# Scattering the experts' rows to token order, and moving the middle variance and the rank products beside the next item's embedding

## The chip, the cores and the metric

One core of one Trainium2 chip runs the kernel. The metric is the device time of one execution in microseconds (us). Engines are named as in the profile: PE (TensorE), DVE (VectorE), ACT (ScalarE), POOL (GpSimd), and SP, which here only issues DMAs.

## What is computed

128 images of 176x208 go through a small vision network in float32. `h` is a row of 128 features for each of 144 tokens an image (143 patches and a class token), 18432 tokens in all.

```python
h = tok(x)                        # patches @ W + b, class token, positions
h = h + L0_attn(layernorm(h))     # projections, 4-tap causal convolution, linear scan
                                  #   s[t] = a * s[t-1] + d[t], gates, output projection
h = h + L0_ffn(layernorm(h)):
    x = LN(x + mean over r of repeat(pool(x, 2**r)) @ mr_w[r])   # "middle" normalization
    x = LN(x + sum over v of alpha[v] * gelu(x @ mv_w[v]))
    logits = x @ gate_w + gate_b;  top 2 of 8 experts, softmax of the two
    moe = sum over the two: weight * (gelu(x @ w1[e] + b1[e]) @ w2[e] + b2[e])
    x = LN(x + moe)
h = h + L1_attn(layernorm(h))     # 8 heads, window of 32 tokens to each side
h = h + L1_ffn(layernorm(h))      # one of 16 matrices per image, chosen by the mean
```

## The kernel before

The kernel is three stages in a row. All engines have instruction streams of their own, written out by hand and joined by semaphores. Features lie on the 128 partitions and tokens along the free dimension. An item is 4 images, 576 tokens (`T`), and there are 32.

**Stage A** (`a_tensor`, `a_scalar`, `a_vector`, `a_pool`, `a_sync`) runs a software pipeline without loops: `a_steps` calls each engine's `step(x, y, z, w)` with four successive items. x is embedded and gets its projections, y its scan's end, output projection and middle normalization, z its three views, third normalization and routing. Four double banks of PSUM (`A0`, `A1`, `B0`, `B1`) hold all products, so the order on PE is also the order in which banks come free. In a step, `embed` (24 matmuls, L508) comes near the start. `ranks` (L543 to 555) and the middle variance of y (L656 to 660) come at the end, around the last `unit_in`. `ranks` counts with 14 small matmuls how many earlier tokens chose each expert. On DVE the routing of z is a chain of small operations on 96x48 numbers (`route_first` to `route_weights`, L934 to 1009), placed between the operations of x: `route_ranks` and `route_slots` turn ranks into row numbers (`slot`, `slot_i`), `route_weights` makes the two softmax weights. Row numbers and weights of all items also stay in SBUF, in `slots` and `weights`. POOL adds a residual, multiplies for x (`drive`, L1015, twice), adds (L1031), and then scatters z's rows, 12 indirect DMAs of 96 rows of 128 floats (L1039), into the DRAM tensor `expert_in`, where each expert has a region. ACT changes its function table at four places of a step and names the gelu table twice.

**Stage B** (`b_tensor`, `b_scalar`, `b_vector`, `b_sync`) runs over 152 blocks of 256 rows of one expert each, in a hardware loop with four blocks a round. `b_sync` loads rows and the expert's weights (`w_blk`) and stores the results in block order to `expert_out`. PE turns the next block's rows (L1156), does four hidden products (L1165) and the outputs (L1174). ACT does gelu. DVE copies the turned rows to `x_t` (L1273) and adds the bias into `rows_out` (L1281). Ahead of the loop DVE works out in a chain where each token's two results will lie (`out_rows`, L1261 to 1269).

**Stage C** (`c_tensor`, `c_scalar`, `c_vector`, `c_pool`, `c_sync`) is again a pipeline without loops, `step(v, w, x, y, z)` with five items. For v, SP loads `h1c` and `x2c`, DVE copies v's row numbers to `place` (L1829), and POOL gathers the two results of each token with 12 indirect DMAs (L1466), multiplies them with their weights (L1474) and adds the two (L1479, `ysum`). PE turns the sum (L1509) at the end of the step. w is normalized, giving `xq` (L1961), x has attention in nine units (scores L1538, exponentials L1752, turned L1555, values L1568 and L1580), y and z the last layer. Keys are evicted by ACT at L1737.

## Time and profile before

| what | value |
|---|---|
| time, median of 3 runs | 3334.4 us (3329.47 to 3344.37) |
| the profiled execution's own time | 3318.28 us |
| its span, first to last instruction | 3316.4 us |
| mean granted TensorE clock | 0.901 of full |
| PE busy | 2775.0 us (84%) |
| DVE busy | 1901.2 us (57%) |
| ACT busy | 1843.2 us (56%) |
| POOL busy | 1134.6 us (34%) |
| moved by DMA | 287.14 MB, mean 87 GB/s |

Times in a profile are of one execution. "Busy" is time inside instructions; a wait is booked as idle time ahead of an instruction, with what ended it in brackets. A clock of 1.00 is 2.4 GHz and 0.50 is 1.2 GHz.

### The profile page before, as it was taken

What the parts mean: (1) busy time and instruction counts of PE and PEld (TensorE: products, weight loads), DVE (VectorE), ACT (ScalarE), POOL (GpSimd) and SP (SyncE); (2) the same over time, 40 slices, a digit from 0 to 9 for tenths busy, and PEclk for the clock granted to TensorE, in tenths of its full rate; (3) what the DMA queues carried; (4) which work ended last, traced back from release to release, by engine and by line L of the source; (5) the groups of instructions that cost most, each with busy time, mean ns of one, the idle gap of its engine ahead of it and who ended that gap; (6) DMA issues with size and microseconds to landing.
All of it is one profiled execution on the core that took longest, in us unless ns stands there. A gap on an engine that the chain in (4) does not pass through costs nothing.

```text
span 3316.4 us, 69976 instructions
## 1 busy us (share of the span) xinstructions
PE 2775.0 (84%) x25687; PEld 2181.5 (66%) x25687; DVE 1901.2 (57%) x4527; ACT 1843.2 (56%) x3725; POOL 1134.6 (34%) x964
## 2 busy tenths in 40 slices
PE   6999999999999859999996677877788777877787
PEld 4766666666666549999995456655566555655565
DVE  4878878878788742222221355655565555655566
ACT  4777777777777734444443345544454444544454
POOL 1454555655555530000002533333333333333310
PEclk9999999999999979999998688887888888878888
DMA  3222222222222137777774111111111111111110
GB/s 119 88 84 72 96 83 72 101 78 75 100 76 73 42 114 228 228 230 227 230 228 140 34 40 41 29 41 44 44 40 27 43 44 43 40 28 44 44 30 26
DMA packets 139758, 287.14 MB, mean 87 GB/s; under 512 B 25440, under 2 KB 82784, under 8 KB 135392
## 3 DMA queue, kind: packets, MB, share of 16 engines
q1 hardware_dynamic: 114912, 245.68, 22.9%
q0 software_dynamic: 24576, 37.80, 4.2%
q8 instruction: 177, 2.90, 0.4%
q14 instruction: 93, 0.76, 0.1%
HBM read 215.08 MB, written 68.29 MB: 85 GB/s over the span
## 4 chain that ended last, share of the span: by engine, by line
PE 47%; issue 7%; another core or an unknown queue 4%; DVE 3%; ACT 1%; POOL 1%; DMA 0%; SPq 0%; DVEq 0%; ACTq 0%; POOLq 0%
PE psum L1174 8%; PE psum L1165 8%; PE psum L1538 7%; PE psum L1498 5%; PE psum L1555 3%; PE psum L1568 3%; PE psum L1523 2%; PE psum L1503 2%; PE psum L1580 2%; DVE qdiag L1837 1%; PE psum L1598 1%; PE psum L1156 1%; PE psum L1546 1%; DVE inv L1852 1%
## 5 line engine op out<-in xcount | busy, mean ns | idle before, releaser
L1466 POOL DMA_INDIRECT ycho<-expert_out,place x384 | 367.5, 957 | 1417.4 <-DVE place L1829 1309.7
L1208 ACT ACTIVATE hid<-psum,w_blk 128x256 f32<-128x256 f32 x608 | 269.1, 474 | 326.2 <-PE psum L1165 326.2
L1039 POOL DMA_INDIRECT expert_in<-rows,slot_i x384 | 392.3, 1022 | 133.2 <-issue 111.6
L1852 DVE RECIPROCAL inv<-psum 128x64 f32<-128x64 f32 x288 | 159.5, 554 | 464.7 <-remote 385.9
L1538 PE MATMUL psum<-keys,qdiag 64*64 64x80 f32 x4608 | 281.4, 256 | 124.1 <-issue 123.7
L1752 ACT ACTIVATE ex<-psum,smin 128x80 f32<-128x80 f32 x1152 | 282.2, 332 | 142.9 <-DVE smin L1845 135.8
L1538 PEld LDWEIGHTS psum<-keys,qdiag 64*64 64x64 f32 x4608 | 214.8, 148 | 211.1 <-issue 195.7
L502 PE MATMUL psum<-xn,w_in 128*128 128x288 f32 x1024 | 311.1, 429 | 39.6 <-DVE xn L861 10.2
L1174 PE MATMUL psum<-w_blk,hid 128*128 128x128 f32 x2432 | 296.6, 275 | 0.0
L1568 PE MATMUL psum<-ex_t,pair_ones 128*32 128x64 f32 x4608 | 137.8, 244 | 189.6 <-DVE half L1853 124.0
L1165 PE MATMUL psum<-x_t,w_blk 128*128 128x256 f32 x1216 | 289.5, 381 | 2.4 <-DMA w_blk<-w_exp_in 2.4
L1174 PEld LDWEIGHTS psum<-w_blk,hid 128*128 128x128 f32 x2432 | 283.7, 192 | 0.1
L1760 ACT ACTIVATE ex_t<-psum 128x512 f32<-128x512 f32 x288 | 174.1, 605 | 174.6 <-PE psum L1555 92.2
L502 PEld LDWEIGHTS psum<-xn,w_in 128*128 128x128 f32 x1024 | 187.8, 196 | 111.4 <-DVE xn L861 23.5
L1015 POOL TENSOR_TENSOR unit<-unit 128x576 f32<-128x576 f32 x64 | 119.4, 1865 | 393.7 <-ACT unit L671 276.2
L1568 PEld LDWEIGHTS psum<-ex_t,pair_ones 128*32 128x32 f32 x4608 | 86.5, 119 | 240.8 <-DVE half L1853 128.5
L1165 PEld LDWEIGHTS psum<-x_t,w_blk 128*128 128x128 f32 x1216 | 212.8, 191 | 34.4 <-DMA w_blk<-w_exp_in 2.8
L1273 DVE COPY x_t<-psum 128x256 f32<-128x256 f32 x152 | 64.6, 425 | 230.5 <-PE psum L1156 230.5
L508 PE MATMUL psum<-xin,w_tok 128*128 128x286 f32 x768 | 194.0, 409 | 2.5 <-DVEq L469 2.5
L1555 PE MATMUL psum<-cst,ex 128*128 128x128 f32 x1152 | 182.0, 280 | 7.5 <-ACT ex L1752 5.2
L1281 DVE TENSOR_TENSOR rows_out<-psum,w_blk 128x256 f32<-128x256 f32 x152 | 64.6, 425 | 215.7 <-PE psum L1174 215.7
L805 DVE SCALAR_TENSOR_TENSOR acc<-pj,taps,acc 128x576 f32<-128x576 f32 x192 | 182.3, 950 | 0.1
(247 smaller groups left out, 5848.5 us busy)
## 6 DMA issues: line engine op xcount, KB each, us to landing
w_blk<-w_exp_in SPq DMA_DIRECT2D x152, 578.0 KB, 3.8
xin<-x_in SPq DMA_DIRECT2D x32, 1716.0 KB
rows_in<-expert_in SPq DMA_DIRECT2D x152, 128.0 KB, 2.3
expert_out<-rows_out SPq DMA_DIRECT2D x152, 128.0 KB, 3.0
h_dram<-h SPq DMA_DIRECT2D x32, 288.0 KB
x_dram<-x SPq DMA_DIRECT2D x32, 288.0 KB
h1c<-h_dram SPq DMA_DIRECT2D x32, 288.0 KB
x2c<-x_dram SPq DMA_DIRECT2D x32, 288.0 KB
```

Source lines behind the costliest of these rows:

```text
L502: last = nc.tensor.matmul(bank[:, g, 0:T2], w, two(src)[:, g, :], start=True, stop=True)
L508: last = nc.tensor.matmul(bank[:, g, 0:2 * NPATCH], w_tok[:, k, :], xin[x.s][:, k, g * 2 * NPATCH:(g + 1) * 2 * NPATCH], start=(k == 0), s ...
L1039: pool.indirect_dma_start(out=expert_in[:, :], out_offset=bass.IndirectOffsetOnAxis(ap=slot_i[z.s][:, n:n + 1], axis=0), in_=rows[z.s][:, ...
L1165: nc.tensor.matmul(HB[b.s][c % HK], w_blk[b.q][:, c * 128:(c + 1) * 128], x_t[b.s][:], start=True, stop=True).then_inc(hid_done[b.s], 1)
L1174: last = nc.tensor.matmul(YB[b.s][:, t * 128:(t + 1) * 128], hid[b.s][:, c, t * 128:(t + 1) * 128], w_blk[b.q][:, FF + c * D:FF + (c + 1) ...
L1208: nc.scalar.activation(hid[b.s][:, c, :], HB[b.s][c % HK], ACT.Gelu_apprx_tanh, bias=w_blk[b.q][:, FF + FC * D + c:FF + FC * D + c + 1]).t ...
L1466: pool.indirect_dma_start(out=ycho[x.s][:, k, :], out_offset=None, in_=expert_out[:, :], in_offset=bass.IndirectOffsetOnAxis(ap=place[x.s] ...
L1538: nc.tensor.matmul(bank[at, b * QK:(b + 1) * QK], qdiag[at, u * UB + b, :, :].rearrange("p j q -> p (j q)"), keys[at, m, key_range(qb)], s ...
L1555: done = nc.tensor.transpose(XB[0:KW, b * 128:(b + 1) * 128], ex[u][:, b, :], C("ident"))
L1568: nc.tensor.matmul(sum_bank()[at], pair_ones[:, j, :], ex_t[u % RING][:, :, t * PH + j * QB:t * PH + (j + 1) * QB], start=(j == 0), stop=( ...
L1752: done = nc.scalar.activation(ex[u][:, b, in_window(qb)], score_bank(u)[:, b * QK:(b + 1) * QK], ACT.Exp, bias=smin[u % RING][:, b:b + 1], ...
L1852: v.reciprocal(inv[:], sum_bank()).then_inc(head_step, 1)
```

## The change

Two things are changed.

*Results in token order.* A row in `expert_in` is now 132 floats: the 128 features, the token's number, a number for its first chosen expert, and the two weights. Stage B scales each row with its own weight (`shares`) and DVE works out where it goes (`dest`: token number, plus the number of tokens if it is the second choice; rows that fill up a block go to spare rows). POOL scatters the two halves of a block to `expert_out` by indirect DMA (`b_pool`), in place of SP's store. Stage C then loads an item's two sets of results with two plain DMAs from SP and only adds them. `slots`, `weights`, `out_rows`, `place`, the 12 gathers and the weighted product are gone.

*Order in stage A.* The middle variance moves to the start of the next step, ahead of the embedding. The rank products go between the two halves of the embedding, in a bank of their own turn. The running sum of picks over the six groups is now a scan on DVE (`upto_g`), so `ranks` has 6 matmuls in place of 14. DVE does `route_slots` and `route_weights` in the next step after the first normalization. The scatter follows in that step, six DMAs ahead of and six behind the first `drive`. ACT names four tables a step in place of five, and does the first normalization's exponentials ahead of the third normalization's square. The pipeline gets one step more.

```diff
@@ ranks
-                pe.wait_ge(route_step, z.upto(ROUTE, 13))
+                pe.wait_ge(route_step, z.upto(ROUTE, 15))
...
-                for g in range(NG - 1):
-                    nc.tensor.matmul(dst[:, g + 1:NG, :], C("ones")[0:G, 0:G],
-                                     picks[z.s][:, g:g + 1, :].to_broadcast([G, NG - 1 - g, E]),
-                                     start=False, stop=False)
+                nc.tensor.matmul(dst, C("ones")[0:G, 0:G], by_group(upto_g[z.s][:]), start=False, stop=False)
@@ a_tensor step
+                if z:
+                    pe.wait_ge(squared2, z.upto(1, 1))
+                    if y:
+                        pe.wait_ge(unit_act, y.upto(8, 4))
+                    project(A1, C("mean"), sqf[:]).then_inc(variance2, 1)
                 if x:
                     pe.wait_ge(x_landed[x.s], 16 * x.n + 16)
...
+                    embed(x, 0, B0)
+                if w:
...
+                    ranks(w, A0)
+                if x:
+                    embed(x, 1, B0)
@@ a_vector step
+                if z:
+                    v.wait_ge(rstd2, z.upto(1, 1))
+                    v.scalar_tensor_tensor(out=x1[:], in0=pre[:], scalar=V("ln1_g"), in1=rf[:],
+                                           op0=ALU.mult, op1=ALU.mult).then_inc(x1_step, 1)
+                if w:
+                    route_ranks(v, w, A0)
                 if y:
                     tap(y, 1, 1)
...
                     v.tensor_tensor(two(xn1[x.s][:]), both(A0), two(ra[:]), ALU.mult).then_inc(normed, 1)
+                if w:
+                    route_slots(v, w)
+                    route_weights(v, w)
@@ a_pool step
                     pool.tensor_tensor(res[x.s][:], h0[x.s][:], xn1[x.s][:], ALU.add).then_inc(res_done, 1)
+                if w:
+                    scatter_ready(w)
+                    scatter(w, 0)
+                if x:
                     drive(x, 0)
+                if w:
+                    scatter(w, 1)
+                if x:
                     drive(x, 1)
@@ stage B, POOL
+            def store(b):
+                hold(pool, dest_ready[b.s], b.k + 1)
+                hold(pool, rows_out_ready[b.s], b.k + 1)
+                for c in range(CB):
+                    pool.indirect_dma_start(
+                        out=expert_out[:, :], out_offset=bass.IndirectOffsetOnAxis(ap=dest[b.s][:, c:c + 1], axis=0),
+                        in_=rows_out[b.s][:, c, :], in_offset=None).then_inc(block_stored[b.s], 16)
@@ stage B, DVE
+            def shares(b):
+                expert = w_blk[b.q][:, WCOLS - 1:WCOLS]
+                first_pick = rows_in[b.q][:, :, FIRST]
+                v.wait_ge(r_landed[b.q], 16 * b.i + 16)
+                v.wait_ge(w_landed[b.q], 16 * b.i + 16)
+                v.tensor_scalar(second[b.s][:], first_pick, expert, float(tokens), ALU.not_equal, ALU.mult
+                                ).then_inc(share_step[b.s], 1)
+                v.scalar_tensor_tensor(out=share0[b.s][:], in0=first_pick, scalar=expert, in1=rows_in[b.q][:, :, W0],
+                                       op0=ALU.is_equal, op1=ALU.mult).then_inc(share_step[b.s], 1)
+                v.scalar_tensor_tensor(out=share1[b.s][:], in0=first_pick, scalar=expert, in1=rows_in[b.q][:, :, W1],
+                                       op0=ALU.not_equal, op1=ALU.mult).then_inc(share_step[b.s], 1)
...
+                if not b.first():
+                    v.wait_ge(block_stored[b.s], 16 * CB * b.k)
+                v.wait_ge(share_step[b.s], 4 * b.k + 3)
+                v.tensor_tensor(share[b.s][:], share0[b.s][:], share1[b.s][:], ALU.add).then_inc(share_step[b.s], 1)
+                v.tensor_tensor(dest[b.s][:], rows_in[b.q][:, :, TOKEN], second[b.s][:], ALU.add
+                                ).then_inc(dest_ready[b.s], 1)
+
             def block(b, final=False):
                 if not final:
                     take_in(following(b))
+                shares(b)
                 v.wait_ge(y_done[b.s], b.k + 1)
...
+                v.tensor_tensor(sums_y[b.s][:], YB[b.s].rearrange("p (c d) -> p c d", c=CB),
...
+                for c in range(CB):
+                    last = v.tensor_scalar(rows_out[b.s][:, c, :], sums_y[b.s][:, c, :], share[b.s][:, c:c + 1], None,
+                                           ALU.mult)
+                last.then_inc(rows_out_ready[b.s], 1)
@@ stage C, SP
+                if x.old(2):
+                    hold(sp, ysum_step, x.upto(1, -1))
+                for choice in range(2):
+                    sp.dma_start(ycho[x.s][:, choice, :, :].rearrange("p g d -> p (g d)"),
+                                 expert_out[choice * tokens + (2 * x.n + x.s) * T:choice * tokens + (2 * x.n + x.s + 1) * T,
+                                            :].rearrange("(p g) d -> p (g d)", g=NG)).then_inc(gathered[x.s], 16)
@@ stage C, POOL
-                for k in range(2 * NG):
-                    pool.indirect_dma_start(
-                        out=ycho[x.s][:, k, :], out_offset=None, in_=expert_out[:, :],
...
-                pool.tensor_tensor(ycho[x.s][:], ycho[x.s][:], w.unsqueeze(2).to_broadcast([G, 2 * NG, D]), ALU.mult
-                                   ).then_inc(ysum_step, 1)
...
+                pool.tensor_tensor(ysum[:], ycho[x.s][:, 0, :, :], ycho[x.s][:, 1, :, :], ALU.add).then_inc(ysum_step, 1)
```

## Rows read from the trace of the kernel before

**Rows 1.** The page, part 1: busy us, share of the span, instructions.

```profile
PE 2775.0 (84%) x25687; PEld 2181.5 (66%) x25687; DVE 1901.2 (57%) x4527; ACT 1843.2 (56%) x3725; POOL 1134.6 (34%) x964
```

**Rows 2.** Busy time by stretch, columns: window: us, five engines' busy, PEclk, DMA share, GB/s.

```profile
0.00:1219.64 1219.64, 1057.66 (x4777) 785.36 (x4778) 941.59 (x1911) 863.19 (x1196) 621.28 (x516) 0.96 0.24 82
1219.64:1789.30 569.66, 569.59 (x3950) 522.25 (x3950) 128.32 (x303) 270.34 (x609) 0.00 (x0) 1.00 0.73 226
...
1835.97:1877.52 41.55, 30.73 (x391) 23.67 (x392) 14.63 (x37) 16.68 (x45) 18.92 (x16) 0.73 0.11 30
1877.52:3221.36 1343.84, 1033.58 (x15363) 788.46 (x15362) 749.79 (x2081) 642.83 (x1739) 466.07 (x406) 0.83 0.14 38
3221.36:3252.71 31.35, 31.35 (x545) 24.14 (x547) 24.08 (x71) 21.92 (x61) 0.00 (x0) 1.00 0.07 21
```

**Rows 3.** Timeline of one item in C: start, us, instruction, [idle before <- releaser].

```profile
2387.98 1.03 POOL L1466 DMA_INDIRECT ycho<-expert_out,place  x1 [0.30 <-issue]
...
2397.01 0.56 DVE L1852 RECIPROCAL inv<-psum 128x64 f32<-128x64 f32 x1 [7.25 <-remote]
...
2401.21 0.74 ACT L1737 ACTIVATE keys<-psum,col 128x576 f32<-128x576 f32 x1 [10.85 <-remote]
```

**Rows 4.** Busy time in the same item: the stall, and all 12 gathers.

```profile
2390.50:2404.00 13.50, 2.34 (x33) 1.62 (x34) 1.17 (x4) 0.74 (x1) 9.29 (x11) 0.63 0.18 47
...
2386.73:2401.57 14.84, 5.20 (x78) 3.70 (x76) 4.12 (x13) 3.17 (x8) 11.49 (x12) 0.75 0.36 102
```

**Rows 5.** Timeline around the last item but one.

```profile
3221.01 0.66 PE L1509 MATMUL psum<-cst,ysum 96*128 96x96 f32 x6
...
3226.54 0.74 ACT L1737 ACTIVATE keys<-psum,col 128x576 f32<-128x576 f32 x1 [0.22 <-PE psum L1515]
```

**Rows 6.** POOL's addition as a group (busy, mean ns | idle), and C's first sum.

```profile
L1479 POOL TENSOR_TENSOR ysum<-ycho 96x768 f32<-96x768 f32 x32 | 57.9, 1808 | 2.5
...
1818.44 1.19 PE L1509 MATMUL psum<-cst,ysum 96*128 96x96 f32 x6 [29.21 <-POOL ysum L1479]
```

**Rows 7.** Busy time in one step of A, and during its 12 scatters.

```profile
609.75:644.69 34.94, 31.86 (x150) 23.59 (x149) 28.47 (x58) 26.54 (x38) 19.72 (x16) 1.00 0.25 85
...
617.39:632.94 15.55, 14.17 (x65) 9.96 (x64) 10.86 (x15) 12.32 (x18) 12.20 (x12) 1.00 0.48 174
```

**Rows 8.** Timeline of one step of A, in order of time.

```profile
629.49 0.82 DVE L868 SCALAR_TENSOR_TENSOR x<-psum,shift,rf 128x576 f32<-128x576 f32 x1 [1.19 <-issue]
...
635.03 0.20 DVE L937 TENSOR_TENSOR logit<-psum,row 96x48 f32<-96x48 f32 x1 [1.29 <-remote]
...
638.22 1.40 POOL L1015 TENSOR_TENSOR unit<-unit 128x576 f32<-128x576 f32 x1 [3.85 <-DVE unit L811]
...
640.39 0.34 PE L549 MATMUL psum<-picks,cst 96*96 96x48 f32 x2 [1.40 <-ACT unit L671]
...
644.44 0.20 DVE L986 TENSOR_TENSOR logit<-cand,pick 96x48 f32<-96x48 f32 x1
...
646.07 0.16 DVE L998 CAST slot_i<-slot 96x12 int32<-96x12 f32 x1
...
647.45 2.70 POOL L1015 TENSOR_TENSOR unit<-unit 128x576 f32<-128x576 f32 x1 [7.83 <-ACT unit L671]
...
649.07 1.10 DVE L1009 TENSOR_TENSOR weights<-wexp,weights 96x6 f32<-96x6 f32 x1
...
653.07 1.34 DVE L816 TENSOR_TENSOR_SCAN unit<-decays,unit 128x576 f32<-128x576 f32 x1
```

**Rows 9.** Four blocks of B; DVE's eviction; a scatter's landing; the weights' landing.

```profile
1505.33:1520.26 14.93, 14.93 (x106) 13.70 (x105) 3.40 (x8) 7.08 (x16) 0.00 (x0) 1.00 0.73 227
...
L1281 DVE TENSOR_TENSOR rows_out<-psum,w_blk 128x256 f32<-128x256 f32 x152 | 64.6, 425 | 215.7 <-PE psum L1174 215.7
...
1211.33 2.19 DMA expert_in<-rows,slot_i
...
w_blk<-w_exp_in SPq DMA_DIRECT2D x152, 578.0 KB, 3.8
```

More of the change, by code:

```diff
@@ L58 @@
 E2 = 16
+RW = D + 4
+TOKEN, FIRST, W0, W1 = D, D + 1, D + 2, D + 3
 EPS = 1e-5
@@ L215, in build @@
         quad = sb("quad", [128, QH])
-        place = [sb(f"place{s}", [G, 2 * NG], I32) for s in range(2)]
         loaded = sem("loaded")
@@ L351, in still @@
                 step(*[Item((t - k) // 2, (t - k) % 2) if 0 <= t - k <= LAST else None for k in range(LAG + 1)])
-            for t in range(LAST + LAG):
+            for t in range(LAST + LAG + 1):
                 still(t)
@@ L400, in a_prep_vector @@
             step(v.memset(chosen[:], 0.0))
+            step(v.memset(within[:], 1.0))
+            settle()
+            step(v.memset(by_group(within[:])[:, 0, :], 0.0))
             for s in range(2):
@@ L503, in project, with embed @@
                 return last
[L505 to L511 removed]
+            def embed(x, g, bank):
+                for k in range(KC):
+                    last = nc.tensor.matmul(bank[:, g, 0:2 * NPATCH], w_tok[:, k, :],
+                                            xin[x.s][:, k, g * 2 * NPATCH:(g + 1) * 2 * NPATCH],
+                                            start=(k == 0), stop=(k == KC - 1))
+                last.then_inc(tok_done, 1)
             def unit_in(x, u, bank):
@@ L685, in step @@
             def step(x, y, z, w):
-                act.preload_act_table_set("gelu_apprx_tanh_and_others")
+                if z:
+                    act.wait_ge(variance2, z.upto(1, 1))
+                    nc.scalar.activation(two(rf[:]), both(A1), ACT.Ln, bias=eps_col[:, 0:1]).then_inc(logvar2, 1)
+                    act.wait_ge(logvar2, z.upto(1, 1))
+                    nc.scalar.activation(rf[:], rf[:], ACT.Exp, scale=-0.5).then_inc(rstd2, 1)
+                if y or z:
+                    act.preload_act_table_set("gelu_apprx_tanh_and_others")
                 if y:
@@ L707, in step @@
                     nc.scalar.activation(two(ra[:]), both(B1), ACT.Ln, bias=eps_col[:, 0:1]).then_inc(logvar0, 1)
-                if z:
-                    act.wait_ge(centered3, z.upto(1, 1))
-                    nc.scalar.activation(two(sqf[:]), both(A1), ACT.Square, bias=shift1[:, 0:1]).then_inc(squared3, 1)
                 if x:
@@ L1016, in drive, with scatter_ready, scatter @@
                                    ).then_inc(drive_ready, 1)
+            def scatter_ready(w):
+                if w.old(2):
+                    pool.wait_ge(scattered[w.s], 16 * 2 * NG * w.n)
+                pool.tensor_scalar(rows[w.s][:, :, TOKEN], C("token")[0:G, :], float((2 * w.n + w.s) * T), None,
+                                   ALU.add).then_inc(token_ready, 1)
+                hold(pool, token_ready, w.upto(1, 1))
+                hold(pool, rows_ready, w.upto(2, 2))
+                hold(pool, slots_ready, w.upto(1, 1))
+                hold(pool, route_step, w.upto(ROUTE, ROUTE))
+            def scatter(w, choice):
+                for g in range(NG):
+                    n = choice * NG + g
+                    pool.indirect_dma_start(
+                        out=expert_in[:, :],
+                        out_offset=bass.IndirectOffsetOnAxis(ap=slot_i[w.s][:, n:n + 1], axis=0),
+                        in_=rows[w.s][:, g, :], in_offset=None).then_inc(scattered[w.s], 16)
             def step(x, y, z, w):
@@ L1053, in build @@
         mem_b = ExitStack()
-        WCOLS = FF + FC * D + FC + D
+        WCOLS = FF + FC * D + FC + D + 1
         w_blk = [sb(f"w_blk{q}", [128, WCOLS], F32, mem_b) for q in range(BR)]
-        rows_in = [sb(f"rows_in{q}", [128, CB, D], F32, mem_b) for q in range(BR)]
+        rows_in = [sb(f"rows_in{q}", [128, CB, RW], F32, mem_b) for q in range(BR)]
+        share0, share1, share = (pair(n, [128, CB], F32, mem_b) for n in ("share0", "share1", "share"))
+        unused, unused_step = sb("unused", [128, CB], F32, mem_b), sem("unused_step")
+        second, dest = pair("second", [128, CB], F32, mem_b), pair("dest", [128, CB], I32, mem_b)
+        sums_y = pair("sums_y", [128, CB, D], F32, mem_b)
         rows_out = pair("rows_out", [128, CB, D], F32, mem_b)
@@ L1421, in c_sync @@
         def c_sync(sp):
+            for s in range(2):
+                sp.wait_ge(block_stored[s], 16 * CB * (NB // 2))
             def load(x):
```

263 lines of the change are left out of this document (101 added, 162 removed).

## The prediction

> **What bounds the kernel now.** I first read the page's busy table [rows 1], then the busy time by stage [rows 2]. The kernel is three stages in a row. The embedding and routing stage (A) takes 1220 us. The expert stage (B) takes 570 us with PE busy all of it at full clock. The attention stage (C) takes 1527 us, and in its long middle stretch PE is busy only 77% at a granted clock of 0.83. So A is nearly full, B is PE-bound, and the idle time lies in C.
>
> To see what stops C, I read the timeline of one of its 32 items [rows 3]. POOL issues the 12 gathers of the experts' rows one by one, from 2386.73 to 2401.57. Meanwhile DVE waits 7.25 us and ACT 10.85 us for something the profile can't name ("remote"), although the matmuls that their code waits for had ended. In the 13.5 us from 2390.5 PE is busy 2.34 us, at clock 0.63, and the DMA engines 18% [rows 4]: bandwidth isn't the limit. From 2404 on all engines run. The last item but one is the one to compare with [rows 2, 5]: nothing is loaded or gathered beside it, ACT's wait for the same key projection is 0.22 us, and it takes 31.35 us at clock 1.00 with PE full. The 29 before it take 1343.84 / 29 = 46.34 us each. These 15 us an item carry the prediction. The clean item lacks the plain loads as well as the gathers, but the stall outlasts the loads by some 10 us, so I put it on the gathers.
>
> **Stage C.** The gathers, POOL's product with the weights and DVE's row numbers go. In come two plain loads of 288 KB on SP's queue, ahead of the expert weights and the output store (four issues instead of two), with a wait for POOL's addition of two items ago, long done. POOL's addition stays, 1.81 us [rows 6]. The loads start some 2 us into a step and their sum is needed at its end, 25 us later; that distance hides them, and without it each step would pay their landing of some 5 us. Late next is PE itself. The new step is the clean one (31.35), the six transposes that it lacks (0.66 [rows 5]), and 0.4 for DVE standing behind POOL's addition: in A a small operation took 1.10 us beside a POOL product instead of 0.16 [rows 8], so the bounds of this term are 0 and 1.5. That makes 32.4 us, between 32.0 and 33.9. 29 x (46.34 - 32.4) = **404 us**.
>
> The first step (41.55 us [rows 2]) has the same gathers beside less work; I take 30 us, a gain of 11. At the start of C the last block's matmuls end at 1789.3 [rows 2], and after the first gathers PE gets their sum at 1818.44 [rows 6]. In the new kernel: rows ready about 1790.3, two scatters issued by 1792.9, landed 1794 (2.19 us [rows 9]), four loads 5 us (twice the 578 KB that land in 3.8 us [rows 9]), addition 1.8, so PE starts at about 1803. Gain 15.
>
> **Stage B.** A block is 14.93 / 4 = 3.73 us and PE is busy throughout [rows 9]. SP's store becomes two scatters on POOL, which is otherwise idle: 2 x (1.03 + 0.30 between two) = 2.7 us, or 3.2 at 1.6 each [rows 3]. DVE's two operations of 0.425 us become about eleven: the same two, two multiplications of half their size (0.21) and seven on 128x2 (0.16, from the cast of `slot_i` [rows 8]): 0.85 + 0.42 + 1.1 = 2.4 us, with 0.1 for each of six dependent waits 3.0 us, under 3.73. They fit: the scaled rows are ready 1.0 us after the output matmuls, the next copy to `x_t` is due 1.95 us after them, and both things that PE waits for are early by about 1 us. A new wait stands in DVE's queue, for the stores of two blocks ago, ahead of `dest`; behind it are the sum and the next copy, for which PE waits. Its loop is: scaled rows, two issues, landing, `dest`, sum: 1.2 + 2.19 (idle) to 5 (under load) + 2.1 = 5.5 to 8.3 us against two blocks, 7.46. I take **0**, with bounds 0 and 0.3 us a block, 46 us.
>
> **Stage A.** A step is 34.9 us: PE busy 31.9, DVE 28.5, POOL 19.7 [rows 7]. DVE never idles from the logits to the mixing, and waits only among the normalizations (four times 1.2 to 2 us; 1.19 and 1.29 stand in [rows 8]). So its busy stretch plus the latency of the normalizations is the step. From the busy stretch four slot operations (0.20), the copy `slots` (0.16, gone) and the weights (0.16 + 1.10) move to where 1.19 us are idle: -2.2 us there, +0.3 here. The reduction to `newly` (0.23) becomes a scan of 48 elements, taken as equal. ACT loses one of five table loads (1.28), and its first exponentials no longer stand behind another item's square: 0.5 us of the latency. PE loses its 1.40 us gap before the ranks and 8 of 14 rank matmuls (two take 0.34) [rows 8], which lie beside DVE's work. The new waits on DVE, for the variance and for the ranks ahead of the first tap, come after PE is through with both. The middle variance and the ranks stand between parts of the embedding (6.0 us), which hides their latency; with that cover gone it would be 3 us.
> Against it: the 12 scatters, 15.55 us on POOL [rows 7], now stand before and between the two `drive` products. Starting about 6 us before the logits (635.03), six end 1.7 after them, before the first product (at 3.2). Six more end at 12.4, the second product (2.70) at 15.1. DVE scanned its result at 18.0 before [rows 8] and now wants it at 15.7. The addition behind it (2.05) ends 17.2, wanted at 17.1. So POOL is just in time; I charge 0.5 us. Together -2.2 + 0.3 - 0.5 + 0.5 = -1.9, of which I take **-1.5** since little slack is left on PE; bounds -2.6 and 0. 31 steps make 47 us. The pipeline's added step holds only the last item's ranks and scatter, which ended the stage before: 0, bounds 0 and 3.
>
> **The sum.** The profiled execution took 3318.3 us. 3318.3 - 404 - 11 - 15 - 47 = 2841. The median before (3334.4) lies 16 us above it; I add half, since part of that scatter should go with the stalls: **2848 us**.
>
> **The rivals.**
> 1. *The stall isn't the gathers'* but comes with the plain loads, which double. Against it: the stall goes on at a DMA share of 18%. Then steps stay near 46 us: 2848 + 404 = 3250. Chance 0.05. The Trainium skill ("SBUF — State Buffer", Who interferes with whom) says that DMA never contends with a compute engine and that PE and ACT wait on nobody; by that rule the gathers could not be the cause and this rival would hold. The trace speaks against the rule [rows 3, 4].
> 2. *B becomes bound by the store loop* or by DVE, from a landing above 5 us on; at +1 us a block 152 us, about 3000. For it: margins of only 1 us. Chance 0.08.
> 3. *DVE's longer loop body is fetched anew* in each of 36 rounds: if a fetch costs a landing, 2.19 us, 79 us, about 2927. Against it: PE's own loop, far longer, runs without a gap now [rows 9]. Chance 0.03. The Trainium skill ("Runtime: NRT & Kernel Launch", Instruction fetch mechanics) says that a taken branch to outside a small window must fetch its target first.
> 4. *POOL becomes late in A*: at 1.58 us an issue for all 12 instead of 1.30, the second product is 3 us late and steps take 36.5: 47 + 50 more, about 2945. Chance 0.05.
> 5. *Slower than before*: scatters in B stop all engines as gathers do in C. 15 us for 12 is 1.2 us each; 304 of them make 375 us, nearly the whole gain, and from 1.6 us each on the kernel is slower, about 3350. Against it: during 12 scatters in A PE is busy 14.17 of 15.55 us, during 12 gathers 5.20 of 14.84 [rows 7, 4]. Chance 0.04.
>
> That the change doesn't do what it says would be gathers left in C; the diff leaves none. The forecast itself has 0.72, and a gain in A down to PE's own work (below 2780) 0.03.
>
> **How the numbers follow.** Down: 34 us (A at its bound), 12 (steps of 32.0), 8 (no half offset), 14 for the first steps: 2780. Up: 47 (no gain in A), 43 (steps of 33.9), 22 (half of B's bound): 2960. The range 2780 to 2960 holds the forecast and rivals 3 and 4, 0.80. A measurement of this kernel can tell 0.5% from no change. All cases but the fifth are faster, and of it 0.01 lies within 0.5%: faster 0.96, same 0.01, slower 0.03.
>
> **What would show it.** C: items 32 to 33 us apart, no "remote" waits, clock near 1.00. B: 3.73 us a block, DVE busy about 2.4 of it. A: steps of 33 to 34 us, the first `drive` product behind the sixth scatter. It is wrong if waits of 5 us and more stay in C, or PE idles in B.

## The result, and the profile after

The changed kernel takes 3048.55 us (median of 4 runs, 3045.51 to 3051.19), the kernel before in the same comparison 3335.14 us: a ratio of 0.914, 95% interval 0.9115 to 0.916. It is faster by 8.6%, but 200 us slower than the 2848 us predicted, and 89 us above the range. The profiled execution has a span of 3046.2 us.

Busy us, share of the span and instructions, and the granted clock in 40 slices, of the kernel after (to hold against [rows 1]):

```profile
PE 2704.1 (89%) x25431; PEld 2101.5 (69%) x25431; DVE 2036.1 (67%) x5663; ACT 1778.9 (58%) x3693; POOL 1106.7 (36%) x884
...
PEclk9999999999999999779999999989999999999998
```

The busy time by stretch, columns as in [rows 2]: stage A, stage B, the start of C, its first step, the 29 steps, the clean item, the rest.

```profile
0.00:1330.89 1330.89, 1078.25 (x4522) 795.80 (x4522) 923.92 (x1863) 821.26 (x1164) 758.10 (x548) 0.92 0.23 75
1330.89:1971.51 640.62, 606.01 (x3950) 520.40 (x3950) 314.90 (x1516) 256.80 (x609) 288.45 (x302) 1.00 0.65 202
1971.51:2003.21 31.70, 11.04 (x28) 6.32 (x27) 7.67 (x16) 4.14 (x6) 6.04 (x5) 0.57 0.40 118
2003.21:2031.53 28.32, 25.57 (x389) 19.41 (x388) 14.00 (x36) 16.42 (x45) 1.80 (x1) 0.94 0.13 42
2031.53:2952.43 920.90, 912.07 (x15363) 704.88 (x15362) 715.99 (x2052) 634.37 (x1739) 52.33 (x29) 1.00 0.20 55
2952.43:2983.77 31.34, 31.34 (x545) 24.15 (x547) 24.09 (x71) 21.87 (x61) 0.00 (x0) 1.00 0.07 21
2983.77:3046.20 62.43, 39.87 (x660) 30.52 (x649) 35.53 (x111) 24.03 (x72) 0.00 (x0) 0.85 0.10 32
```

Against [rows 2] this settles where the time went and came from:

| stretch | before | after | difference | predicted |
|---|---|---|---|---|
| stage A | 1219.64 | 1330.89 | +111.3 | -47 |
| stage B | 569.7 | 640.6 | +71.0 | 0 |
| start of C, to its first sum on PE | 29.1 | 14.2 | -15 | -15 |
| first step of C | 41.55 | 28.32 | -13.2 | -11 |
| 29 steps of C | 1343.84 | 920.90 | -422.9 | -404 |
| the rest of C (the clean item is equal) | 63.7 | 62.4 | -1.3 | 0 |
| sum | | | -270 | -477 |

(The start of C runs from the last output matmul, at 1971.51, to PE's first L1544, at 1985.68. From there to the first step it is 17.5 us in both kernels.) Stage C is as forecast: 31.8 us a step, PE busy 912 of 921 us, clock 1.00. The whole miss lies in the other two stages.

**Stage A.** A step is counted from POOL's addition of one item's residual to the next item's. From the fifth item on the steps are 38.8 us long on average; they were 35.2. The stage's granted clock falls from 0.96 to 0.92. POOL and DVE in one of them, start, us, instruction, idle time before it:

```profile
608.24 0.92 POOL L1034 DMA_INDIRECT expert_in<-rows,slot_i  x1 [0.30 <-issue]
609.46 7.69 POOL L1034 DMA_INDIRECT expert_in<-rows,slot_i  x1 [0.30 <-issue]
617.45 0.92 POOL L1034 DMA_INDIRECT expert_in<-rows,slot_i  x1 [0.30 <-issue]
...
620.83 1.42 POOL L1018 TENSOR_TENSOR unit<-unit 128x576 f32<-128x576 f32 x1
...
609.66 0.75 DVE L807 SCALAR_TENSOR_TENSOR pj<-unit,zproj 128x576 f32<-128x576 f32 x1
...
611.55 0.45 DVE L823 TENSOR_SCALAR unit<-unit 128x576 f32<-128x576 f32 x1
611.92 1.54 DVE L817 SCALAR_TENSOR_TENSOR acc<-pj,taps,acc 128x576 f32<-128x576 f32 x2
613.38 1.34 DVE L828 TENSOR_TENSOR_SCAN unit<-decays,unit 128x576 f32<-128x576 f32 x1
614.64 0.79 DVE L842 SCALAR_TENSOR_TENSOR x<-pre,col,rf 128x576 f32<-128x576 f32 x1
...
616.28 0.44 DVE L800 TENSOR_TENSOR h<-psum,posb 128x286 f32<-128x286 f32 x1
...
622.28 2.55 DVE L828 TENSOR_TENSOR_SCAN unit<-decays,unit 128x576 f32<-128x576 f32 x1 [4.47 <-POOL unit L1018]
...
627.09 3.38 PE L525 MATMUL psum<-acc,w_out 128*128 128x288 f32 x8 [4.04 <-DVE acc L834]
```

The ninth of the twelve scatters takes 7.69 us in place of 0.92. So the second `drive` product (620.83) is late, DVE's scan waits 4.47 us for it, and PE's output projection 4.04 us for DVE. The ninth scatter has a mean of 6.2 us over the 32 items, the fifth 1.4, the others 0.9 to 1.6; in 29 items one of them, mostly the ninth, takes 7.2 to 8.3. It ends 0.87 us after DVE begins L800, which reads PSUM and one tile of SBUF, and in all 28 held scatters with an L800 in them it is so, within 0.01 us. From 609.66 on DVE has worked without a gap, almost all of it on operations with two inputs in SBUF. On the page the same chain stands as groups:

```profile
L1034 POOL DMA_INDIRECT expert_in<-rows,slot_i x384 | 563.8, 1468 | 173.9 <-issue 103.0
...
L525 PE MATMUL psum<-acc,w_out 128*128 128x288 f32 x256 | 118.9, 638 | 122.0 <-DVE acc L834 122.0
...
L828 DVE TENSOR_TENSOR_SCAN unit<-decays,unit 128x576 f32<-128x576 f32 x64 | 121.7, 1901 | 134.0 <-POOL unit L1018 134.0
```

Up to the last item's addition this makes about 92 of the 111 us. The other 19 come after it: one more held scatter, and then the last two items' scatters with little other work beside them.

**Stage B.** A block takes 640.6 / 152 = 4.21 us in place of 569.7 / 152 = 3.75. PE is busy 606 of the 641 us and waits for ACT's gelu; ACT waits for PE. Waits from 1400 to 1900, us in total, times, longest:

```profile
ACT hid L1234 <- PE psum L1191: 295.7, 145, 3.2
...
PEld psum L1191 <- ACT hid L1234: 67.7, 116, 1.2
```

Each of the two seems to wait for the other. The timeline shows what is late. One block, and then one of the experiment without scatters (below):

```profile
1601.06 0.95 POOL L1163 DMA_INDIRECT expert_out<-rows_out,dest  x1 [0.30 <-issue]
1601.10 1.46 PE L1191 MATMUL psum<-x_t,w_blk 128*128 128x256 f32 x6
1602.62 1.74 ACT L1234 ACTIVATE hid<-psum,w_blk 128x256 f32<-128x256 f32 x4 [2.84 <-PE psum L1191]
...
1602.06 1.89 PE L1199 MATMUL psum<-x_t,w_blk 128*128 128x256 f32 x8
1602.70 1.77 ACT L1242 ACTIVATE hid<-psum,w_blk 128x256 f32<-128x256 f32 x4 [1.97 <-PE psum L1199]
```

With a scatter beside it ACT's first gelu starts 1.52 us after PE's hidden products, without one 0.64 us. Over all 152 blocks this distance has a mean of 1.11 us in the kernel after, and of 0.64 us both in the kernel before and without scatters. The 0.47 us more, 152 times, are the stage's 71 us.

### The profile page after: what moved, and what is told of

The parts are those of the page before. It is cut to its first block, busy times and chain, and to the rows that moved or that the text cites. A ratio compares the mean times of both kernels' runs of the same rounds, so it can differ in the third digit from the quotient of the medians.

```text
span 3046.2 us, 71218 instructions
## 1 busy us (share of the span) xinstructions
PE 2704.1 (89%) x25431; PEld 2101.5 (69%) x25431; DVE 2036.1 (67%) x5663; ACT 1778.9 (58%) x3693; POOL 1106.7 (36%) x884
## 4 chain that ended last, share of the span: by engine, by line
PE 52%; DVE 3%; ACT 2%; issue 1%; POOL 1%; DMA 1%; another core or an unknown queue 0%; SPq 0%; DVEq 0%; POOLq 0%; ACTq 0%
PE psum L1191 10%; PE psum L1200 9%; PE psum L1533 6%; PE psum L1573 6%; PE psum L1590 5%; PE psum L1603 3%; PE psum L1550 2%; PE psum L1538 2%; PE psum L1615 2%; PE psum L1558 2%; PE psum L1633 1%; PE psum L1182 1%; ACT hid L1234 1%; PE psum L1581 1%; PE psum L1583 1%
## 5 line engine op out<-in xcount | busy, mean ns | idle before, releaser
L1034 POOL DMA_INDIRECT expert_in<-rows,slot_i x384 | 563.8, 1468 | 173.9 <-issue 103.0
L1163 POOL DMA_INDIRECT expert_out<-rows_out,dest x304 | 290.9, 957 | 360.8 <-DVE rows_out L1327 308.6
L1516 POOL TENSOR_TENSOR ysum<-ycho 96x768 f32<-96x768 f32 x32 | 57.7, 1804 | 898.3 <-DMA ycho<-expert_out 883.2
L525 PE MATMUL psum<-acc,w_out 128*128 128x288 f32 x256 | 118.9, 638 | 122.0 <-DVE acc L834 122.0
L1573 PE MATMUL psum<-keys,qdiag 64*64 64x80 f32 x4608 | 222.4, 236 | 1.2 <-ACT keys L1772 0.8
L1573 PEld LDWEIGHTS psum<-keys,qdiag 64*64 64x64 f32 x4608 | 175.5, 133 | 61.6 <-issue 41.4
L828 DVE TENSOR_TENSOR_SCAN unit<-decays,unit 128x576 f32<-128x576 f32 x64 | 121.7, 1901 | 134.0 <-POOL unit L1018 134.0
L525 PEld LDWEIGHTS psum<-acc,w_out 128*128 128x128 f32 x256 | 72.8, 297 | 159.9 <-issue 133.9
L1321 DVE TENSOR_TENSOR sums_y<-psum,w_blk 128x256 f32<-128x256 f32 x152 | 64.6, 425 | 174.1 <-PE psum L1200 172.1
L513 PEld LDWEIGHTS psum<-xin,w_tok 128*128 128x128 f32 x768 | 145.7, 193 | 39.5 <-DVEq L475 2.6
```

What stands on the lines that cost most here:

```text
L513: last = nc.tensor.matmul(bank[:, g, 0:2 * NPATCH], w_tok[:, k, :], xin[x.s][:, k, g * 2 * NPATCH:(g + 1) * 2 * NPATCH], start=(k == 0), s ...
L525: last = nc.tensor.matmul(bank[:, g, 0:T2], w_out[:, c, :], two(acc[y.s][c][:])[:, g, :], start=(c == 0), stop=(c == 1))
L1034: pool.indirect_dma_start(out=expert_in[:, :], out_offset=bass.IndirectOffsetOnAxis(ap=slot_i[w.s][:, n:n + 1], axis=0), in_=rows[w.s][:, ...
L1163: pool.indirect_dma_start(out=expert_out[:, :], out_offset=bass.IndirectOffsetOnAxis(ap=dest[b.s][:, c:c + 1], axis=0), in_=rows_out[b.s][ ...
L1573: nc.tensor.matmul(bank[at, b * QK:(b + 1) * QK], qdiag[at, u * UB + b, :, :].rearrange("p j q -> p (j q)"), keys[at, m, key_range(qb)], s ...
```

## Experiments

Each experiment is one run, except the last kernel, which has four. The kernel before took 3319 to 3341 us beside them, by the chip that they ran on; differences of some 20 us between two experiments are therefore read from the stages and not from the total.

**What holds the ninth scatter.** The first suspect was the `delta` operation (L823), one input and 0.45 us for 576 elements, which lies in both of the long scatters (the fifth and the ninth).

```diff
-                v.tensor_scalar(unit[x.s][DELTA[c]][:], unit[x.s][DELTA[c]][:], 1.0, 2e-4, ALU.add, ALU.max
-                                ).then_inc(delta_ready, 1)
+                v.scalar_tensor_tensor(out=unit[x.s][DELTA[c]][:], in0=unit[x.s][DELTA[c]][:], scalar=1.0,
+                                       in1=least[:], op0=ALU.add, op1=ALU.max).then_inc(delta_ready, 1)
```

> Changed from the kernel after: the `delta` operation of both units (L823, 0.45 us, one SBUF input) becomes a two-input operation with a constant tile (about 0.75 us); nothing is left out. In the kernel after, the ninth scatter of each step takes 7.2 to 8.3 us instead of 0.92, the fifth 1.75, and a `delta` operation lies in both. Theory P: that fast single-input operation shuts POOL's descriptor writing out, and the two-input operations that follow without a gap keep it out. Then the ninth scatter takes 1.0 to 1.3 us, the second `drive` comes some 6 us earlier, steps of stage A fall from 38.8 to 33.5 to 35 us, and the kernel takes about 2910 us. Rival Q: any unbroken row of DVE operations does it, or the ninth scatter waits for room in the queue. Then it stays at 7 us or more, DVE has 0.6 us more a step, and the time is 3045 to 3065 us.

Measured: 3055.9 us, steps of 39.2 us, as the rival has it. POOL in a step of this kernel:

```profile
617.11 8.14 POOL L1036 DMA_INDIRECT expert_in<-rows,slot_i  x1 [0.30 <-issue]
```

Theory P falls: with `delta` as a two-input operation the scatter is held as long as before. Its rival had two causes in one, any unbroken row of DVE or a full queue; the next two experiments part them.

**POOL's order.** The same kernel after, with all scatters behind both products.

```diff
                 if w:
                     scatter_ready(w)
-                    scatter(w, 0)
...
                     drive(x, 0)
-                if w:
-                    scatter(w, 1)
...
                     drive(x, 1)
...
+                if w:
+                    scatter(w, 0)
+                    scatter(w, 1)
```

> Changed from the kernel after: on POOL the 12 scatters stand behind both `drive` products and the addition into `acc`, in one row, as before the change, but a step later than there; nothing is left out. Theory: POOL's place for the scatters is what costs stage A its 111 us. The second `drive` product then waits for ACT alone, the 4.5 us waits of DVE for it go, steps take 34 to 35.5 us instead of 38.8, and the kernel takes 2910 to 2950 us. If other parts of the change made the steps longer (the ranks between the embedding's halves, the middle variance), they stay at 37 us or more and the time is above 3000 us.

Measured: 2937.65 us, steps of 34.8, as expected, and stage A (columns as in [rows 2]):

```profile
0.00:1215.95 1215.95, 1035.54 (x4522) 755.73 (x4522) 930.94 (x1863) 822.38 (x1164) 722.24 (x548) 0.97 0.24 83
```

So POOL's order costs the whole 111 us. And something new: the second `drive` product, 1.4 us elsewhere, takes 5.54 us. POOL and DVE there:

```profile
633.90 5.54 POOL L1018 TENSOR_TENSOR unit<-unit 128x576 f32<-128x576 f32 x1 [4.70 <-DVE unit L823]
...
637.38 0.80 DVE L817 SCALAR_TENSOR_TENSOR acc<-pj,taps,acc 128x576 f32<-128x576 f32 x1
638.10 0.44 DVE L800 TENSOR_TENSOR h<-psum,posb 128x286 f32<-128x286 f32 x1
638.47 1.59 DVE L817 SCALAR_TENSOR_TENSOR acc<-pj,taps,acc 128x576 f32<-128x576 f32 x1
```

The product is no DMA, so it can't be waiting for room in a queue, and it is held by the same row of DVE operations. It ends at 639.44, 1.34 us after L800 begins, about its own length, and now DVE's next two-input operation is the one that is held: 1.59 us in place of 0.80. One engine at a time, and the change of hands comes at L800.

**Gaps in DVE's row.** If that is so, any operation that leaves POOL room will do.

```diff
+            def port_gap(k):
+                v.tensor_reduce(gap[:, k:k + 1], C("ones")[:, 0:128], AX_X, ALU.add)
+                v.tensor_reduce(gap[:, k + 4:k + 5], C("ones")[:, 0:128], AX_X, ALU.add)
...
                     silu(x, 1)
+                    port_gap(0)
...
                     delta(x, 1)
+                    port_gap(1)
...
                     tap(x, 1, 2)
+                    port_gap(2)
                     tap(x, 0, 0)
+                    port_gap(3)
                     states(x, 0)
```

> Changed from the kernel after: in stage A four pairs of small one-input reductions (128x128 to 128x1, result unused) are put among the row of DVE operations in which the ninth scatter lies (behind silu, delta, and two taps); nothing is left out, DVE does about 2 us more a step. Theory R (formed after e1 and e2): POOL cannot read SBUF while DVE runs operations with two SBUF inputs one after the other without a gap; a one-input operation of 0.2 us lets it in. The ninth scatter, 6.2 us on average and 7.2 where it is held, then takes under 3 us; the ones behind it may each wait 1 to 2 us. The second drive comes 2 to 4 us earlier, DVE is 2 us longer, and the time is 2960 to 3050 us. If the scatter waits for something else (room in its queue, a landing), it keeps its 7 us, and the time is 3060 to 3110 us.

Measured: 2931.4 us, 117 us less than the kernel after, with 60 us more of work on DVE in stage A (984 in place of 924). The steps are 34.3 us. That is below the range I gave it (2960 to 3050). The ninth scatter of a step, the first reduction in it, and the group of all scatters in the kernel:

```profile
632.30 1.95 POOL L1043 DMA_INDIRECT expert_in<-rows,slot_i  x1 [0.30 <-issue]
...
633.38 0.27 DVE L839 TENSOR_REDUCE gap<-cst 128x1 f32<-128x128 f32 x1
...
L1043 POOL DMA_INDIRECT expert_in<-rows,slot_i x384 | 416.2, 1084 | 172.1 <-issue 102.9 <-DVE rows L1021 68.9 <-DVE acc L818 0.3
```

The scatter ends at 634.25, again 0.87 us after the operation that lets it in has begun. The scatters' mean falls from 1468 to 1084 ns, with POOL's order untouched. This is the cause of the longer steps: POOL gets no access while DVE's operations with two inputs in SBUF follow each other closely. The kernel before had such a place too, and a reciprocal of 0.16 us stood in it, from `route_weights`, which the change has moved away. DVE of the kernel before, behind the start of POOL's product at 647.45 [rows 8]:

```profile
647.60 1.35 DVE L816 TENSOR_TENSOR_SCAN unit<-decays,unit 128x576 f32<-128x576 f32 x1
648.87 0.16 DVE L1007 RECIPROCAL weights<-wsum 96x6 f32<-96x6 f32 x1
```

There the product ended at 650.15, and it was DVE's next operation, L1009, that took 1.10 us [rows 8]. The prediction took that 1.10 as a price for DVE in stage C; it did not ask what the same pair of rows means for POOL in stage A.

The Trainium skill ("SBUF — State Buffer", Who interferes with whom) has the rule: a DVE instruction with two SBUF inputs contends with a GpSimd instruction that reads SBUF, and the second to start is blocked until the first ends. The trace agrees, with one thing more: the block lasts over a whole row of instructions (7.69 us, no single one over 1.34). The next one of DVE begins before POOL gets in.

**The scatters split.** Six ahead of the first product, six behind the addition.

```diff
                 if x:
                     drive(x, 0)
-                if w:
-                    scatter(w, 1)
-                if x:
                     drive(x, 1)
...
+                if w:
+                    scatter(w, 1)
```

> Changed from the kernel after: six scatters stay ahead of the first drive product, the other six move behind the second one and the addition into acc; nothing is left out. By theory R the ninth scatter no longer stands ahead of the second drive product in the row of two-input operations. e2, with all 12 behind, has steps of 34.8 us with a wait of 3.4 us for the logits while scatters run. With the split the drives are in time and fewer scatters stand beside the normalizations: steps of 33.5 to 34.5 us and 2895 to 2930 us. If the scatters cost the same wherever they stand, steps stay at 34.8 and the time at 2938 us.

Measured: 2904.1 us, steps of 34.15 us, as expected. Stages A and B:

```profile
0.00:1191.22 1191.22, 1039.25 (x4522) 769.26 (x4522) 941.73 (x1863) 822.33 (x1164) 730.02 (x548) 0.95 0.25 84
1191.22:1827.64 636.42, 605.10 (x3950) 519.87 (x3950) 314.96 (x1516) 257.52 (x609) 289.43 (x302) 1.00 0.63 203
```

POOL and DVE still hold each other up in it: the second `drive` product, 1.57 us on average in the kernel after, takes 4.91. But it starts in time, because no scatter stands between it and the first product.

**What stage B pays for.** First without the scatters:

```diff
+            def store(b):
+                hold(sp, rows_out_ready[b.s], b.k + 1)
+                sp.dma_start(expert_out[bass.DynSlice(b.n * BLK, BLK), :].rearrange("(p c) d -> p (c d)", c=CB),
+                             rows_out[b.s][:].rearrange("p c d -> p (c d)")).then_inc(block_stored[b.s], 16)
...
-            b_pool(pool)
```

> Changed from the kernel after: in stage B the two scatters of a block on POOL are left out, and SP stores the block in one plain DMA in block order; DVE's eleven operations a block stay. Left out: the token order, so stage C reads rows of other tokens. Stage B takes 641 us in the kernel after, 570 us before the change. Theory S: the scatters delay PE's results on their way to ACT and DVE. Then stage B takes 570 to 580 us and the kernel about 2980 us. Rival D: DVE's nine more operations make x_t or rows_out late. Then stage B stays at 635 to 645 us and the time at 3040 to 3055 us.

Then with the scatters, but few operations on DVE:

```diff
-                shares(b)
+                v.tensor_scalar(second[b.s][:], second[b.s][:], float(2 * BLK), None, ALU.add).then_inc(share_step[b.s], 1)
...
+                v.tensor_scalar(dest[b.s][:], second[b.s][:], 0.0, None, ALU.add).then_inc(dest_ready[b.s], 1)
                 v.wait_ge(y_done[b.s], b.k + 1)
-                v.tensor_tensor(sums_y[b.s][:], YB[b.s].rearrange("p (c d) -> p c d", c=CB),
+                v.tensor_tensor(rows_out[b.s][:], YB[b.s].rearrange("p (c d) -> p c d", c=CB),
```

> Changed from the kernel after: in stage B the two scatters a block stay, but their targets are counted on (two operations of DVE on 128x2) and the share of each row is left out, so DVE has four operations a block in place of eleven. Left out: the weights and the token order. Theory S (the scatters cost stage B its time): it stays at 630 to 645 us and the kernel at 3035 to 3055 us. Rival D (DVE's operations): stage B takes 570 to 580 us, the kernel about 2980 us.

Measured: 2979.35 us and 3017.1 us. Stage B alone, the first line without scatters, the second with them and few operations:

```profile
1327.29:1897.17 569.88, 569.88 (x3950) 522.94 (x3950) 314.21 (x1516) 270.19 (x609) 0.00 (x0) 1.00 0.73 227
...
1324.78:1936.94 612.16, 607.04 (x3950) 518.21 (x3950) 181.32 (x606) 257.56 (x609) 289.02 (x302) 1.00 0.66 212
```

Without scatters the stage takes 569.9 us, as before the change, and DVE has all its operations (nine or eleven a block): theory S holds, and DVE's operations alone cost nothing. But with scatters and few operations it is 612, not 641: of the 71 us, 42 are the scatters' with little else, and 28 come only where both are there. Neither theory had foreseen that sum. That delayed results of PE leave DVE less time, so that its operations count, is my reading; no run separates it. The distance from PE to ACT of above is 0.96 us here. A scatter in this stage costs 42 / 304 = 0.14 us by itself, and 71 / 304 = 0.23 us with the small operations beside it.

**What the gathers did in stage C.** The forecast rested on the gathers as the cause of the stalls. Put back, for nobody:

```diff
+            def extra(x):
+                if x.old(1):
+                    pool.wait_ge(spared, 16 * 2 * NG * (2 * x.n + x.s))
+                for k in range(2 * NG):
+                    pool.indirect_dma_start(
+                        out=spare[:, k, :], out_offset=None, in_=expert_out[0:2 * tokens, :],
+                        in_offset=bass.IndirectOffsetOnAxis(ap=at_rows[:, k:k + 1], axis=0)).then_inc(spared, 16)
...
                 if v:
+                    extra(v)
                     weighted_sum(v)
```

> Changed from the kernel after: in stage C POOL again issues 12 indirect gathers an item of 96 rows of 512 bytes, ahead of its addition, into a tile that nothing reads; the plain loads and all else stay, nothing is left out. Theory G (my forecast): the gathers themselves stop the engines, whoever wants their data. Steps go from 31.8 to 45 to 47 us and the time from 3048 to 3450 to 3520 us. Rival (the stall of the kernel before came from waiting for their data, or from the weighted product): steps stay at 31.8 to 34 us, the time under 3120 us.

In the same place 12 scatters (`out=expert_in[:, :]`, `in_=spare[:]`):

> Changed from the kernel after: in stage C POOL issues 12 indirect scatters an item of 96 rows of 528 bytes into the DRAM rows that stage C no longer reads, at the same place where e7 has its gathers; nothing is left out. Theory I (either direction stalls alike where the engines wait for PE's results, which stages A and B hide in part): steps of 43 to 47 us, time 3400 to 3520 us. Theory D (gathers into SBUF stall, scatters out of it hardly): 0.26 us a scatter as stage B shows ((641 - 570) / 304 = 0.23), so steps of 34 to 36 us, time 3120 to 3190 us.

Plain DMAs of POOL's queue (`pool.dma_start(spare[:, k, :], expert_out[k * G:(k + 1) * G, :])`):

> As e7, but the 12 DMAs an item that POOL issues in stage C are plain ones of 96 rows of 512 bytes, without a list of rows; nothing is left out. Theory Q (what stalls is POOL's own writing of descriptors, for any DMA of its queue): steps of 42 to 46 us, time 3370 to 3480 us, as e7 (44.6 us, 3459 us) has with gathers. Rival (the list of rows, read and worked through one by one, is what stalls): steps of 31.8 to 34 us, time under 3120 us.

And gathers of 32 rows (`spare[0:32, k, :]`, `at_rows[0:32, k:k + 1]`):

> As e7, but each of the 12 gathers an item fetches 32 rows in place of 96; nothing is left out. If the stall goes by rows (descriptors), it is a third of 12.8 us: steps of 36 us, time about 3180 us. If it goes by DMA instructions, steps stay at 43 to 45 us, time 3400 to 3460 us.

Measured: 3459.1, 3442.8, 3075.0 and 3501.6 us. Stage C's steps that have such DMAs beside them, in this order (28 steps; 29 for the plain ones):

```profile
2069.79:3332.01 1262.22, 982.64 (x14833) 739.77 (x14832) 696.01 (x1980) 614.27 (x1679) 359.76 (x364) 0.86 0.18 52
...
2056.02:3314.98 1258.96, 986.73 (x14833) 741.36 (x14832) 693.37 (x1980) 614.10 (x1679) 359.55 (x364) 0.86 0.19 53
...
2055.81:2977.39 921.58, 912.05 (x15363) 704.29 (x15362) 718.17 (x2052) 635.58 (x1739) 220.24 (x365) 1.00 0.26 73
...
2098.98:3374.51 1275.53, 1004.51 (x14833) 751.42 (x14832) 688.96 (x1981) 614.62 (x1679) 343.64 (x364) 0.86 0.15 43
```

| 12 a step | step, us | above 31.76, for each |
|---|---|---|
| gathers of 96 rows | 45.1 | 1.11 |
| scatters of 96 rows | 45.0 | 1.10 |
| plain DMAs, 96 rows | 31.8 | 0.00 |
| gathers of 32 rows | 45.6 | 1.15 |

So the gathers were the cause, and nobody needs to want their data. The direction makes no difference, nor do 32 rows in place of 96: what costs 1.1 us is one indirect DMA instruction on POOL. The same bytes by plain DMAs on the same queue cost these steps nothing (of the 26 us by which that kernel is slower, 12 lie in stage A, 6 in B and 9 in C outside these steps). During the 12 of them PE is busy 5.84 of 6.04 us, during 12 gathers 7.82 of 14.37:

```profile
2509.66:2515.70 6.04, 5.84 (x54) 4.47 (x56) 4.25 (x13) 3.59 (x11) 6.04 (x13) 1.00 0.32 85
...
2530.47:2544.84 14.37, 7.82 (x69) 5.41 (x69) 3.05 (x8) 3.65 (x11) 11.02 (x12) 0.88 0.14 39
```

The waits of the kernel with its gathers back, from 2500 to 2900:

```profile
DVE inv L1899 <- remote: 98.7, 9, 12.9
ACT r L1772 <- remote: 92.9, 9, 11.3
```

Both lines wait for products of PE. What inside the chip holds these results up is open: the runs show only that it comes with the indirect form.

**A better version.** From the split order, POOL now writes each row's target and its own share before each choice's six scatters, so that stage B has two small operations a block in place of five or seven.

```diff
+            def second_choice(w):
+                pool.wait_ge(scattered[w.s], 16 * (2 * NG * w.n + NG))
+                pool.tensor_scalar(rows[w.s][:, :, TOKEN:TOKEN + 2], rows[w.s][:, :, TOKEN:TOKEN + 2], float(tokens), None,
+                                   ALU.add).then_inc(token_ready, 1)
+                pool.tensor_copy(rows[w.s][:, :, SHARE], share2[w.s][:]).then_inc(token_ready, 1)
...
             def shares(b):
                 v.wait_ge(r_landed[b.q], 16 * b.i + 16)
+                v.tensor_copy(share[b.s][:], rows_in[b.q][:, :, SHARE]).then_inc(share_step[b.s], 1)
...
+                v.tensor_copy(dest[b.s][:], rows_in[b.q][:, :, TOKEN + b.s]).then_inc(dest_ready[b.s], 1)
```

> Changed from e6 (2904 us, stage A in steps of 34.15 us, stage B 636 us): POOL writes a row's target and its own weight before each choice's scatter, so that stage B finds both ready and DVE does two small operations a block in place of seven; a row is 524 bytes; nothing is left out. e4 had 612 us of stage B with the scatters, two small operations and no multiplications; e3 had 570 us without scatters. By these, the multiplications kept, stage B takes 612 to 625 us, and if the two more POOL operations an item in stage A cost nothing the time is 2880 to 2895 us. If the multiplications by the share and not the small operations are what e4 saved, stage B stays at 636 us and the time at 2900 to 2910 us.

Measured: 2869.6 us (2866.0 to 2874.4), the kernel before beside it 3319.1: a ratio of 0.864, interval 0.8628 to 0.8657. Its stages A and B:

```profile
0.00:1179.30 1179.30, 1023.49 (x4522) 747.48 (x4522) 958.31 (x1864) 821.85 (x1164) 792.24 (x644) 0.97 0.25 85
1179.30:1790.43 611.13, 598.78 (x3950) 521.43 (x3950) 237.41 (x908) 258.86 (x609) 288.65 (x302) 1.00 0.67 212
```

Stage B takes 611 us with the multiplications, so the small operations and the waits between them are what cost it 25 to 28 us (the distance from PE to ACT is 0.89 us). It beats both kernels, and the expected 2880 to 2895 too. For the latter there are two reasons besides stage B, and neither is explained by the edit: the kernel before is 22 us faster beside this run than beside the split order, and stage A's steps are 33.65 us, at a granted clock of 0.97 where the split order had 34.15 and 0.95. The second product still takes 5.3 us on average.

## Why the prediction was right and wrong

- **What bounds the kernel, stage C: right.** The stall was put on the gathers because it outlasted the loads. The experiments confirm it, and a step came out at 31.8 us, just below its bounds (forecast 32.4, bounds 32.0 to 33.9). It was 0.65 us too high: the 0.4 allowed for DVE behind POOL's addition, and some of the 0.66 for the transposes, since a step is only 0.42 us longer than the clean one. First step and start of C: within 2 us each.
- **Rival 1** (the stall comes with the plain loads) was rightly weighed low. The rule of the Trainium skill named beside it ("SBUF — State Buffer", Who interferes with whom), that PE and ACT wait on nobody and DMA contends with no engine, agrees with the plain DMAs of POOL's queue, which cost 0.00 us. It would have ruled the gathers out, and they cost 1.11 us each; by which path is not shown, so the runs don't say whether the rule or only its use here is wrong.
- **Stage A: the step that failed is the one on POOL.** It said that "POOL is just in time; I charge 0.5 us". It took 1.30 us for every issue, and one of the twelve, the ninth as a rule, takes 7.2 to 8.3. The step came out at 38.8 us and the stage 111 us longer, where 47 us of gain were forecast. The working copied the durations of POOL and DVE from where they stood before, the second product's 2.70 too, and asked nothing of what one engine does to the other in the new places, although [rows 8] showed it from both sides: 2.70 us for a product that takes 1.40, and 1.10 for an operation that takes 0.16. The other half of the error is that I saw the small operations leave DVE's busy stretch as a gain of 2.2 us only. One of them, the reciprocal, was the gap through which POOL came in.
- **The rest of stage A's working comes near as a sum.** With POOL's scatters split, the stage is 28 us shorter than before, and 40 in the best version; the forecast was 47. No run takes the moved variance, the ranks or the DVE operations by themselves, so what each brings is not shown.
- **Rival 4** (POOL late in stage A) is the one that happened, in its place and by its chain: the second product late, the step longer. Its size was off: 1.58 us an issue for all and 36.5 us a step, where one issue is held and a step is 38.8. Its chance of 0.05 was too low for a margin of 0.5 us on 12 instructions.
- **The end of stage A** was put at 0 to 3 us and costs 19. From the last addition on it takes 114 us in the kernel after, 95 in the kernel before and 105 with the split order, so 9 of the 19 are the held scatter once more. Of the other 10, beside the last scatters single waits of DVE and ACT are 5 and 9 us long; that these scatters make them is not shown.
- **Stage B: the term of 0 (bound 46) measured 71.** Rival 2 (store loop or DVE) isn't the cause by itself: without scatters DVE's operations cost nothing. Rival 5's mechanism is: indirect DMAs hold up results of PE. The failed step is that nothing was charged for it: it was priced as all or nothing at 1.2 us each, and set aside because PE is busy 14.17 of 15.55 us during the scatters in stage A [rows 7]. That row does not show what a scatter does where others wait for PE; the scatters in stage C cost 1.1 us each. In stage B it is 0.23 us, 0.14 of it the scatter by itself. That lies between the two prices I had, and neither forecast nor rival had a case for it.
- **Rival 3** (DVE's longer loop fetched anew) did not happen: without the scatters the stage with the same loop on DVE takes 569.9 us.
- **The range** had its upper end from no gain in A, C at its bound, and half of B's bound; rival 4, with steps of 36.5 us, just fitted in. Steps of 38.8 us and blocks of 4.21 us had no place in it, although [rows 8] had two rows of POOL and DVE holding each other up, from which a larger loss could have been priced. (By its own terms the sum comes to 2849 us and not 2848; nothing hangs on it.)

## What to carry to other kernels

Before POOL work is moved beside DVE work, look for rows of DVE operations with two inputs in SBUF without a gap: POOL's next operation or indirect DMA waits for the end of the row, not of an instruction. When small DVE operations are moved away, ask who used the gaps they left. And price an indirect DMA by its stage: 1.1 us each in stage C, where PE, ACT and DVE work from each other's results, 0.14 to 0.23 us in stage B, where PE was busy all the time before (that this is what makes the difference is an inference from two stages); a plain DMA on the same queue, where the rows allow one, costs none of it.

## What the runs showed of the hardware

- In stage C an indirect DMA delays others by its being one, not by its rows: 12 of 32 rows cost 13.8 us a step, 12 of 96 rows 13.3; 12 plain ones of the same bytes as the latter 0.0. It occupies POOL for 0.92 us (96 rows), 0.87 (32 rows) and 0.51 (plain), on average.
- POOL and DVE shut each other out over several instructions: a product of 1.4 us took 5.54, a scatter of 0.92 took up to 8.30. Reductions of a few tenths of a us, a reciprocal of 0.16 us, and additions with one input from PSUM let POOL in; the one-input operations L812 and L823 in the row did not, nor did a 0.20 us addition from PSUM (L993) that overlaps with both of its neighbours.
- Two costs that each look small can need each other: in stage B, DVE's small operations cost 0 us without scatters and 28 with them.
- Stage A alone took 1324 to 1352 us in runs of kernels that differ only behind it, so the 7 us by which the `delta` experiment was slower say nothing.
